# Token mixer with early fusion: the image loads are issued by ScalarE where SyncE issued them

## The reference, cut to what matters

```python
x = layernorm(patches(img)) @ W + b                  # 64 x 196 x 768 -> 256
h = concat([layernorm(x), txt], axis=1)              # 64 x 273 x 256
h = h + attention(layernorm(h))                      # 16 heads of 16
h = h + ffn(layernorm(h))                            # shift, W_r, W_k, W_v
```

## Time and profile before

| | us |
|---|---|
| median of 3 runs | 1543.6 (1542.29 to 1551.1) |
| the profiled execution | 1540.33 |
| its span, first to last instruction | 1538.4 |
| TensorE busy (mean granted clock 0.962) | 1390.7, 90% |
| TensorE weight loads | 1303.4, 85% |
| VectorE busy | 1233.0, 80% |
| ScalarE busy | 1117.4, 73% |
| GpSimd busy | 915.7, 60% |

### The profile page before, as it was taken

How to read it: one execution, slowest core, us unless ns; L and a number is a source line. 1 busy time by engine, 2 the same in 40 slices (tenths; PEclk the granted TensorE clock), 3 DMA queues, 4 the chain that set the end, 5 groups by cost and what they waited for, 6 DMA issues and landing times. The chain is left out here.

```text
span 1538.4 us, 51214 instructions
## 1 busy us (share of the span) xinstructions
PE 1390.7 (90%) x17658; PEld 1303.4 (85%) x17658; DVE 1233.0 (80%) x3104; ACT 1117.4 (73%) x2409; POOL 915.7 (60%) x1593
## 2 busy tenths in 40 slices
PE   5888899999999999999999999899999999999875
PEld 5777888989889899889889889888889889888774
DVE  6878888798888888888788788888889888877642
ACT  4667686788878788877777678767777677766554
POOL 3332464667665576666666565666566656766566
PEclk8799999999999999999999999999999999999878
DMA  6399799899879989879878987879888986997920
GB/s 192 89 168 161 190 161 171 153 168 199 149 188 160 193 165 160 179 153 162 200 162 151 177 158 154 189 132 168 154 169 187 178 136 158 137 177 144 146 58 31
DMA packets 687536, 243.43 MB, mean 158 GB/s; under 512 B 589681, under 2 KB 658353, under 8 KB 687153
## 3 DMA queue, kind: packets, MB, share of 16 engines
q1 hardware_dynamic: 687281, 240.16, 81.0%
HBM read 137.18 MB, written 107.94 MB: 159 GB/s over the span
## 5 line engine op out<-in xcount | busy, mean ns | idle before, releaser
L1797 PE MATMUL bank<-wqkv,xnT 128*128 128x384 f32 x1644 | 330.7, 347 | 12.2 <-DVE xnT L1595 11.1
L1797 PEld LDWEIGHTS bank<-wqkv,xnT 128*128 128x128 f32 x1644 | 280.7, 190 | 21.2 <-DVE xnT L1595 14.9
L1900 PE MATMUL bank<-wtok,xT 128*126 128x258 f32 (+1 forms) x1800 | 249.3, 295 | 7.7 <-DVE xT L1537 7.7
L1425 POOL TENSOR_TENSOR mixp<-mixf,mixp 128x384 fp32r<-128x384 f32 x184 | 185.6, 1020 | 110.9 <-ACT mixp L1770 110.5
L1900 PEld LDWEIGHTS bank<-wtok,xT 128*126 128x126 f32 (+1 forms) x1800 | 236.4, 197 | 11.3 <-DVE xT L1537 9.7
L1691 ACT ACTIVATE arena<-qk,ymask 128x384 f32<-128x384 f32 x368 | 204.4, 611 | 31.7 <-DMA qk<-qkv_dram 16.2
L1607 DVE TENSOR_TENSOR qkvt<-bank,bqkv 128x384 f32<-128x384 f32 x274 | 148.2, 548 | 20.9 <-PE bank L1797 19.7
L1712 ACT ACTIVATE xcols<-xim 84x640 f32<-84x640 f32 (+1 forms) x192 | 120.5, 692 | 58.6 <-DVE xs L1531 30.9
L1440 POOL TENSOR_TENSOR h<-h,r 128x256 f32<-128x256 f32 x138 | 101.2, 740 | 72.0 <-DVE r L1650 70.9
L1369 POOL TENSOR_TENSOR rs<-ve,small 126x1 f32<-126x1 f32 (+1 forms) x192 | 135.1, 703 | 15.0
L1531 DVE TENSOR_REDUCE xs<-xcols 84x14 f32<-84x1792 f32 x64 | 128.5, 2008 | 9.7 <-ACT xcols L1724 8.5
(11 more groups left out here) (118 smaller groups left out, 3183.1 us busy)
## 6 DMA issues: line engine op xcount, KB each, us to landing
qkv_dram<-qkvt SPq DMA_DIRECT2D x138, 384.0 KB, 3.8
xim<-in_x SPq DMA_DIRECT2D x128, 294.0 KB
qk<-qkv_dram SPq DMA_DIRECT2D x46, 768.0 KB, 8.4
arena<-qkv_dram SPq DMA_DIRECT2D x368, 48.0 KB, 4.0
hc<-h_dram SPq DMA_DIRECT2D x45, 384.0 KB, 3.8
out<-h SPq DMA_DIRECT2D x45, 384.0 KB, 5.1
o_dram<-probs SPq DMA_DIRECT2D x108, 96.0 KB
on<-o_dram SPq DMA_DIRECT2D x73, 128.0 KB
```

Of the source, the lines that this page charges most:

```text
L1425: mix_lo.done(P.tensor_tensor(mixp[:, w, 1, kk, :], mixf[:, kk, :], mixp[:, w, 0, kk, :].bitcast(F32), ALU.subtract))
L1797: ins = mm(psum, left(a, k), right(b, k), start=t == 0, stop=t == len(terms) - 1)
L1900: mm(place("tok", 0, t)[0:pr, 0:E + 2], xT[:, a, ch, :, :].rearrange("p i w -> p (i w)")[:, r0:r0 + pr], wtok[:, b, ch, :], start=n == 0, ...
```

## The change

The two transfers of each image's load are issued by ScalarE. The kind `load` keeps its step in the table. For image 0 they stand at the head of ScalarE's program, ahead of its first clearing; for the others they stand at the load's step, behind a wait of ScalarE for its own three copies of the image before, ahead of that step's other work. SyncE keeps `load_rest` at the same steps and no longer waits for `x_cols`. No arithmetic, buffer or step is changed.

```diff
@@ -1221,11 +1221,6 @@
             for s in STEPS:
                 for m in due(s, "load", 0):
-                    after(x_cols, m - 1, 3)
-                    src = x[m:m + 1, :, :, :].rearrange("b c (i r) w -> (b c i) (r w)", r=PS)
-                    for half in range(2):
-                        x_in.done(sp.dma_start(xim[half * 42:half * 42 + 42, :],
-                                               src[:, half * HALF * SIDE:(half + 1) * HALF * SIDE]))
                     load_rest(m)
@@ -1660,6 +1655,13 @@
+            def load_image(m):
+                src = x[m:m + 1, :, :, :].rearrange("b c (i r) w -> (b c i) (r w)", r=PS)
+                for half in range(2):
+                    x_in.done(act.dma_start(xim[half * 42:half * 42 + 42, :],
+                                            src[:, half * HALF * SIDE:(half + 1) * HALF * SIDE]))
+
+            load_image(0)
             act.wait_ge(prep_pool, 5)
@@ -1704,6 +1706,11 @@
+                for m in due(s, "load", 0):
+                    if m > 0:
+                        x_cols.wait(act, m - 1, 3)
+                        settle(act)
+                        load_image(m)
                 for job, (w0, w1) in enumerate(XCUT):
                     for m in due(s, "xcols", job):
```

## The result

| | before | after |
|---|---|---|
| median of 6 runs, us | 1542.44 (1539.96 to 1551.1) | 1572.32 (1560.59 to 1578.48) |
| profiled execution, us | 1540.33 | 1571.54 |

The ratio is 1.0205 [1.0167, 1.0243]: the change makes the kernel 2% slower, by some 30 us. The time lies near the upper end of the range and outside the forecast's own 1546 to 1560; the likeliest figure, 1550, was 22 us too low.

The account below looks back on a forecast made before the run. The prediction took TensorE and short waits passing between all engines to pace the kernel. Its terms, 7.3 + 2 + 1 - 3.8 = +6.5 us, gave 1546.8 against the profiled execution and 1550 us for the median, range 1531 to 1575.

Parts of the forecast that it names:

- ScalarE's issues, +7.3 us: Waits and issues of 63 pairs on ScalarE, partly uncovered, delay the end by 7.3 us, from 0 to 30.
- the 26.5 us of lateness: On ScalarE, uncovered issue time: 9 us at about ten places, none at 18, 17.5 us at 35; from 0 to 60.
- the share of 0.28: Part of TensorE's idle time ended by ScalarE in its three largest rows; translates ScalarE's delay into time at the end.
- The start, +2 and +1 us: First three ScalarE loads in serial work, +2 us (0 to 3); image 0's load ahead of the weights, +1 us.
- The +1 us for the shared DMA engines: At the start, the projection's weights share the DMA engines with image 0: +1 us, from nothing to 3.
- SyncE's relief, -3.8 us: SyncE regains 0.77 us per load, 27.7 us at 36 places, at a share of 0.14: -3.8 us, 0 to -20.
- When the image lands, 0 us: At 11 later places ScalarE reaches the load's step up to 2 us earlier or later than SyncE: 0 us, -5 to +5.
- Rival 1: ScalarE's loads are held by SyncE's issues behind `qk`: 13 to 23 us more, 1563 to 1573, say 1568; chance 0.28.
- Rivals 2 and 3: Rival 2: SyncE is the pace, -20 us, 1524, chance 0.16; rival 3: ScalarE's and SyncE's sides both hidden, 1543, chance 0.14.

Follow-up runs that it names:

- the three pairs: Kernels before and after, each with loads of images 1 to 63 at an eighth, half or all bytes; moving the load costs 0.85%, 1.29% and 2.05%.
- scalar_blanks: Kernel before, images still on SyncE, with the wait and two issues of 42 numbers each added on ScalarE at the 63 places: 1549.57 us, ratio 1.0048.
- first_on_sync: Kernel after, with image 0's load alone given back to SyncE at its old place behind the projection's weights: 1581.74 us, ratio 1.0263 to the kernel before.
- sync_blanks: Kernel after, with SyncE again waiting for the copies and issuing two transfers of 42 numbers at each load of images 1 to 63: 1578.16 us, ratio 1.0246.
- half_each: Kernel before, with the first transfer of each image on SyncE and the second moved to ScalarE: 1544.48 us over 10 runs, ratio 1.0023.
- half_each_first_sync: half_each with both transfers of image 0 on SyncE: 1542.75 us over 12 runs, ratio 1.0037 to the kernel before.
- half_each_and_blank: half_each_first_sync with an issue of 42 numbers on ScalarE ahead of each of its transfers: 1553.04 us over 6 runs, ratio 1.0108 to the kernel before.

## Why the prediction was right and wrong

The direction was right and the sum was a fifth of the loss. The part of the loss that changes with the bytes can be read from the three pairs: 0.85, 1.29 and 2.05% at an eighth, a half and all. A straight line through them gives 0.65% without bytes (10 us) and 1.38% more with all of them (21 us); each of the three points is uncertain by 0.4 to 0.7%, and the growth from the first to the last, 1.2%, by 0.8%. The trace splits the loss in the same way: 9.3 us by the first chunk, 21.8 us after it.

1. **ScalarE's issues, +7.3 us: the product fits, its factors don't.** A pair took 0.74 us in the median (0.93 in the mean, own count), where 0.77 was taken. But the lateness was overestimated. ScalarE's idle time that no other engine ended grew from 2.9 to 12.5 us (own sum of its rows that end by `issue` or by its own copies; 1.9 us lie ahead of its first instruction), by 9.6 where about 25 were to be seen, and behind 31 of the 63 pairs there is no idle time at all. ScalarE's whole idle time grew by 28 us (1538.4 - 1117.4 = 421.0 to 1569.5 - 1120.1 = 449.4), but that is the longer span with the same work and says nothing on the issues. scalar_blanks lost 7.4 us with 12.9 us more of such idle time, and in its trace all of it ahead of the first chunk. So neither the 26.5 us of lateness nor the share of 0.28 is borne out; that their product met the 7.4 us is luck. TensorE's waits in the three rows from which the share came grew by 4.5 us (40.7 to 45.2).

2. **The start, +2 and +1 us: too small.** That the uncovered places cost 0.9 us was right (0.91). The +1 us for the shared DMA engines, bounded at 3 us, was 4.65 us: I bounded it by the load's own time and not by how late the weights could become, on which VectorE's whole preparation hangs. Image 3 began 7.3 us later and not 2 to 3, and the first chunk 9.3 us later. What the 4.65 us alone cost at the end is not shown: first_on_sync takes them back and ends no earlier.

3. **SyncE's relief, -3.8 us: not seen.** TensorE's wait for `on` went up (20.2 to 24.7), not down. SyncE's freed time shows as waits for `yh` and `qkvt`. By the intervals sync_blanks is between 2 us faster and 14 us slower than the kernel after, so 3.8 us are neither shown nor excluded. That the eight `arena` issues at image 38 would meet the load's hold did not come true (1.37 us at most).

4. **When the image lands, 0 us: this step failed, and it holds most of what was missing.** The mark I had set was passed: the wait for `xim` left 20 to 35 us, downward, to 18.0. I had asked only when ScalarE reaches the step of the load, and took the transfer to cost others what it cost before. At image 38 the load in one queue came behind `qk`; from its own queue it went beside `qk`, and `qk` was used 11.5 us after its issue and not 8.0. The bytes cost 21 us by the line above; the prediction had no term for that. The Trainium skill (DMA: Bandwidth & Descriptors, section Issuing engines are not separate DMA queues) says that transfers interleave on the same 16 engines whoever starts them, and that several issuers save only the sequencer's time. The first half agrees with the `qk` rows; I read only the second half, and the 15.1 us landing is what stood in the first.

5. **Rival 1, ScalarE held by SyncE's issues: refuted,** though the measured time, 1572, lies in its interval. A pair went through in 0.32 + 0.41 us while SyncE was held for 6.92, and the mean pair of 0.93 us stays under the 1.2 from which the rival was to decide. The Trainium skill (Perfetto Trace Analysis, section DMA Instruction — HWDGE (DVE, Sync)) has a block that is locked for one issuing sequencer while it makes descriptors, and a note there gives SyncE and ScalarE as the two that the compiler lets issue. This trace does not agree that SyncE's hold is such a lock on ScalarE: ScalarE doesn't meet it. A time that agrees with a rival does not show its mechanism. That the stated range holds 1572 is luck too: its upper end, 1575, was set by this rival.

6. **Rivals 2 and 3** fall with the time. SyncE is not the pace: its 128 issues held it for 78.5 us (own sum; the prediction's 68 counts only the three longest in full), and freeing them brought no gain. ScalarE's issues are hidden in part only.

7. **TensorE's clock: no term.** The prediction priced waits alone. 8.8 of the 31.1 us are TensorE's longer busy time at the lower granted clock (0.957 against 0.962); how much of that comes from the start and how much from the later waits was not separated.

**What stays open.** That the bytes on ScalarE's queue cost time, in a measure that grows with them, is shown by the three pairs. That `qk` lands later where it meets a load is shown as well; that this is the path by which the bytes cost 21 us is argued. The direct test, a load on ScalarE's queue that is held back until `qk` has landed, was not run. half_each speaks against `qk` as the only path: in its trace `qk` lands after up to 14.6 us and four take over 11, nearly as in the kernel after, yet its ten runs cost 0.2%; that trace is of the longest of the ten, 1556.58. At image 38 itself ScalarE's 3.2 us of longer wait don't reach the next chunk: `qk` was issued 29.5 us later than before there, and 29.4 us later for the next one. And scalar_blanks, which moves no image, has 9 us more in the sum of the `qk` landings too, so that sum is no measure by itself. Half of the bytes on ScalarE's queue should cost 10 us by the line; half_each_first_sync, with one issue, cost 5.7 [1.8, 9.7] in all, and half_each_and_blank, with two, 1.08% where the line has 1.34%. Whether the half that stays in SyncE's queue holds back the image's use, and so makes the other half's place harmless, wasn't tried. Why first_on_sync is 0.6% slower than the kernel after (by the intervals 0.1 to 1.0%) isn't known.

## What to carry to other kernels

When a transfer moves to another issuing engine, ask what stood ahead of it in the old queue: the queue's order was a priority, and a transfer that was polite behind an urgent one now shares the engines with it. Price the issues one by one against the ACTIVATE that runs ahead of them: at image 38 one issue of 0.35 us under 0.5 us was free and two were not. Price the serial start by itself: the empty issues lost their time there and next to none later. And when the measured time fits a rival, look for the rival's own mark in the trace before believing it.

## What was not expected of the hardware

- ScalarE's issues had a queue of their own (q10 beside q1), and were not delayed by an issue on SyncE that was held for 6.92 us.
- The same bytes kept the DMA engines busy for the same time (1246 and 1245 us) from one queue or two; the longest landing of a 768 KB transfer rose from 10.8 to 15.1 us.
- At the start 2 x 294 KB issued 0.9 us ahead of the weights delayed the first low part by 4.65 us; with that load given back to SyncE the delay was 0.4 us.
